# A four-stage attention kernel: work of one stage placed inside the end of the stage before

## The chip, the cores and the metric

The kernel runs on one core of one Trainium2 chip, as one program. The metric is the device time of one execution in microseconds; of the kernel before, three executions took 1231.0 to 1233.37 us, with a median of 1232.23.

## What is computed

Four layers follow each other on `x` (8 sequences of 128 tokens, 256 features); `ctx` has the same shape.

```python
# L0: 16 heads of width 8 over the channels; mean and deviation of the attended values
mean, ex2 = attn @ v, attn @ (v * v)
x = instance_norm(x) * sqrt(relu(ex2 - mean * mean)) + mean
# L1: queries from x, keys and values from [ctx, x], 16 heads of width 16, masked
out = rmsnorm(attention @ out_w + out_b + x) * postnorm_w
x = gelu_tanh(out @ w1 + b1) @ w2 + b2 + x                 # width 1024
# L2: two cross attentions on ctx, 16 heads of width 128, one extra learned key and value, then an MLP
for l in (1, 2):
    x = x + attention(layernorm(x), ctx) @ wo[l] + bo[l]
x = x + gelu(layernorm(x) @ fc1 + b) @ fc2 + b
# L3: cross attention on ctx, 16 heads of width 16, masked, then an MLP with gelu_tanh
x = x + attention(layernorm(x), ctx) @ wo + bo
x = x + gelu_tanh(layernorm(x) @ fc + b) @ proj + b
```

## The kernel before, in words

Each engine's program is written from the same lists of events, so that all five agree on the order. `att_order` (line 147) makes the list of an attention with narrow heads (L1 has 64 units, L3 has 32), `wide_order` (252) that of L2's two layers (16 head pairs of 8 units each), `mlp_order` (319) that of an MLP; `late` (229) moves some of VectorE's events behind the next score. The events are:

- `S` scores of a unit in PSUM, VectorE's maximum, ScalarE's Exp; `R` or the reciprocal on VectorE, the product with it on GpSimd (line 1629); `T` transposes of the probabilities (PE line 737 or 815); `PV` values; `OUT` and `WO` the output projection, added on VectorE.
- `dq`, `dk`, `dv`, `pq`, `pk` (L1, L3) and `q`, `k`, `v` (L2): projections.
- `nS`, `nX`, `nT`: the norm. `nS` gathers the statistics and takes the Sqrt on ScalarE (1013), `nX` writes the normalised rows to `XH` (1300, 1302), `nT` transposes two sequences (PE 641), scales them on ScalarE (1027, 1029) and splits them into a rounded part and a remainder in `ht` on VectorE (1316, 1317). `k` counts pairs of sequences, 0 to 3.
- `up` and `down`: the two MLP products of a pair of sequences. `up` is followed by the gelu (1165) and its split on VectorE (1501, 1502), four `up` to one `down`.
- `w`: a weight pack of 1024 columns is taken from the loading buffer `wraw` (two slots) by a cast on ScalarE (1004) and a remainder on VectorE (1266).

TensorE rounds its operands, so `three` (616) makes each dense product of three matmuls, of high and low parts. General products go through two PSUM banks in strict turn (`j_bank`, 603): the third one waits until the first has been read. Weights and operands live in one array `rs`, whose three regions A0, A1 and A2 change hands between the stages.

Between stages the order was this. At the end of an attention the units run out first; then come `nS` and `nX` for the first three pairs of sequences, the first MLP pack, the last `WO`, and `norm_end` (201), that is the last pair's norm and all four `nT`. Only then starts `up` of the first pair. In the MLP the last `down` comes before the next stage's norm is finished in the same way. A `down` waits until all four gelu splits of its pair are there:

```python
pe.wait_ge(m["lo"], (FT // 2) * (c + 1))
```

The last event of SP is one store of the whole output after the last `down`.

## Time and profile before

| | |
|---|---|
| median of three executions | 1232.23 us (1231.0 to 1233.37) |
| the profiled execution's own time | 1233.65 us |
| its span, first to last instruction | 1231.9 us |
| TensorE busy (matmuls) | 1081.0 us, 88% |
| VectorE, ScalarE, GpSimd busy | 747.5, 722.5, 321.1 us |
| mean granted clock of TensorE | 0.952 of full |
| HBM | 36.87 MB read, 1.05 MB written |

Times of rows are counted from the span's start. Busy time of TensorE counts overlapping matmuls once; a bracket behind a row gives the idle time just before it on that engine and what ended it. L0 lasts to some 213 us, the first attention to 372, its MLP to 434, the second stage to 975, its MLP to 1041, the third attention to 1162 and the last MLP to 1226.

### The profile page before, as it was taken

The numbers are of one execution on the slowest core, as the hardware profiler recorded it, in microseconds if no ns is written. First come the engines' busy times: TensorE is split into PE (matmuls) and PEld (weight loads), VectorE is DVE, ScalarE is ACT, GpSimd is POOL, SyncE is SP. The second block draws the span as 40 slices with busy tenths as digits, with TensorE's granted clock in tenths as the row PEclk, the third lists the DMA queues.
The fourth block names the chain that finished last, engine by engine and source line by source line (L and its number), as shares of the span: only waits on it lengthen the run. The fifth ranks groups of instructions, "written<-read, shape, count | busy, mean of one in ns | idle before, by whom it ended". The sixth has DMA issues, their size and how long they took to land. (4 is left out here: it accounts for less than half of the span.)

```text
span 1231.9 us, 23777 instructions
## 1 busy us (share of the span) xinstructions
PE 1081.0 (88%) x8224; PEld 952.6 (77%) x8224; DVE 747.5 (61%) x1763; ACT 722.5 (59%) x2096; POOL 321.1 (26%) x433
## 2 busy tenths in 40 slices
PE   3799995899968899999999989999999687789687
PEld 2577773777748878999999869999998587667487
DVE  4777674687876545555555745555555756666753
ACT  1577774778774346566656556656665433688631
POOL 5234335455440003111111112111111111343210
PEclk9799997999998999999999989999999899899799
DMA  6111110000002111010111111111100111000101
GB/s 198 24 29 44 44 28 34 2 2 1 1 19 75 44 45 40 30 35 34 40 44 65 44 43 44 44 44 44 44 35 19 35 35 35 1 2 2 35 1 35
DMA packets 20364, 43.65 MB, mean 35 GB/s; under 512 B 3347, under 2 KB 10773, under 8 KB 20246
## 3 DMA queue, kind: packets, MB, share of 16 engines
q1 hardware_dynamic: 20246, 42.12, 10.4%
q8 instruction: 68, 1.11, 0.4%
q14 instruction: 50, 0.41, 0.1%
HBM read 36.87 MB, written 1.05 MB: 31 GB/s over the span
## 5 line engine op out<-in xcount | busy, mean ns | idle before, releaser
L1629 POOL TENSOR_TENSOR pt<-pt,prec 128x256 f32<-128x256 f32 (+1 forms) x224 | 180.3, 805 | 647.2 <-DVE prec L1467 513.7
L618 PE MATMUL ps<-rs 128*128 128x256 f32 x480 | 147.0, 306 | 29.5 <-DVE rs L1502 19.4
L1127 ACT ACTIVATE pt<-ps,nmax 128x129 f32<-128x129 f32 x256 | 92.4, 367 | 96.1 <-DVE nmax L1459 95.4
L1266 DVE TENSOR_TENSOR rs<-wraw,rs 128x256 fp32r<-128x256 f32 (+2 forms) x108 | 69.3, 644 | 121.9 <-ACT rs L1004 121.2
L620 PE MATMUL ps<-rs 128*128 128x256 f32 x480 | 139.0, 290 | 0.0
L619 PE MATMUL ps<-rs 128*128 128x256 f32 x480 | 139.0, 290 | 0.0
L618 PE MATMUL ps<-ht,rs 128*128 128x256 f32 (+1 forms) x368 | 128.1, 348 | 2.1 <-ACT rs L1055 1.1
L1078 ACT ACTIVATE pt<-ps,nmax 128x256 f32<-128x256 f32 (+1 forms) x256 | 105.2, 423 | 33.8 <-DVE nmax L1405 25.4
L618 PEld LDWEIGHTS ps<-rs 128*128 128x128 f32 x480 | 95.2, 198 | 35.8 <-DVE rs L1502 12.7
L619 PE MATMUL ps<-ht,rs 128*128 128x256 f32 (+1 forms) x368 | 122.0, 331 | 0.0
L620 PE MATMUL ps<-ht,rs 128*128 128x256 f32 (+1 forms) x368 | 121.5, 330 | 0.0
L619 PEld LDWEIGHTS ps<-rs 128*128 128x128 f32 x480 | 95.5, 199 | 0.0
L1165 ACT ACTIVATE fs<-ps,col 128x256 f32<-128x256 f32 x96 | 40.4, 472 | 93.7 <-PE ps L620 88.1
L620 PEld LDWEIGHTS ps<-rs 128*128 128x128 f32 x480 | 95.2, 198 | 0.0
L1481 DVE SCALAR_TENSOR_TENSOR rs<-ps,col,rs 128x256 fp32r<-128x256 f32 x128 | 61.9, 483 | 46.7 <-ACT rs L1144 46.7
L618 PE MATMUL ps<-rs,ct 128*128 128x256 f32 x288 | 87.9, 305 | 1.3 <-DVE rs L1368 0.9
L1405 DVE TENSOR_REDUCE nmax<-ps 128x2 f32<-128x512 f32 (+1 forms) x96 | 66.2, 690 | 34.7 <-PE ps L729 29.2
L1576 DVE TENSOR_REDUCE nm<-ps 128x2 f32<-128x512 f32 x128 | 81.9, 680 | 8.1 <-PE ps L927 8.1
L806 PEld LDWEIGHTS ps<-fs 128*128 128x128 f32 x512 | 76.2, 191 | 10.2
L619 PE MATMUL ps<-rs,ct 128*128 128x256 f32 x288 | 81.6, 283 | 0.0
L620 PE MATMUL ps<-rs,ct 128*128 128x256 f32 x288 | 81.6, 283 | 0.0
L1206 ACT ACTIVATE pt<-ps 128x512 f32<-128x512 f32 x128 | 73.4, 598 | 12.8 <-PE ps L936 10.8
(198 smaller groups left out, 2989.9 us busy)
## 6 DMA issues: line engine op xcount, KB each, us to landing
wraw<-in_packs SPq DMA_DIRECT2D x55, 512.0 KB, 3.5
bvr<-in_l2rows SPq DMA_DIRECT2D x16, 256.0 KB, 4.6
rs<-rs SPq DMA_DIRECT2D x80, 32.0 KB, 1.9
ht<-rs SPq DMA_DIRECT2D x48, 32.0 KB, 1.9
row<-in_rows SPq DMA_DIRECT2D x2, 640.0 KB, 5.1
out<-X SPq DMA_DIRECT2D x1, 1024.0 KB, 4.5
X<-in_x SPq DMA_DIRECT2D x1, 768.0 KB, 7.5
XH<-in_ctx SPq DMA_DIRECT2D x1, 768.0 KB, 9.3
```

The source lines that it names most:

```text
L618: nc.tensor.matmul(dst, w[0], m[1], start=start, stop=False)
L619: nc.tensor.matmul(dst, w[1], m[0], start=False, stop=False)
L620: return nc.tensor.matmul(dst, w[0], m[0], start=False, stop=stop)
L806: last = nc.tensor.matmul(ps[:, S_BANK + g % 2, b * D:b * D + P + 1], qT[:, hh % 3, 2 * b2 + b, :], kT[:, hh % 3, 2 * b2 + b, :], start=Tr ...
L1078: last = nc.scalar.activation(prob[:, i % 3, h * keys:(h + 1) * keys], ps[:, SCORE_BANKS[ph][i % len(SCORE_BANKS[ph])], h * keys:(h + 1) * ...
L1127: last = nc.scalar.activation(prob[:, g % 3, k * D:k * D + P + 1], ps[:, S_BANK + g % 2, k * D:k * D + P + 1], ACT.Exp, bias=nmax[:, g % 4 ...
L1206: nc.scalar.activation(pt[:, i % L0_PTS, :], ps[:, L0_X[i % len(L0_X)], :], ACT.Exp, scale=Q0_SCALE).then_inc(Z["ex"], 1)
L1266: last = nc.vector.tensor_tensor(dst[1], src, f32(dst[0]), ALU.subtract)
L1405: nc.vector.tensor_reduce(nmax[:, i % 4, 0:nh], ps[:, SCORE_BANKS[ph][i % len(SCORE_BANKS[ph])], :].rearrange("p (h n) -> p h n", h=nh), A ...
L1481: nc.vector.scalar_tensor_tensor(cc[1][:, hd, two, :], ps[:, O_BANK + g % 2, 0:D].rearrange("p (b n) -> p b n", b=2), C(f"L2bv{p // PAIRS ...
L1576: nc.vector.tensor_reduce(nm[:, s % 3, im, 2 * p:2 * p + 2], ps[:, L0_S[i % len(L0_S)], :].rearrange("p (h n) -> p h n", h=2), AX.X, ALU.m ...
L1629: nc.gpsimd.tensor_tensor(pr, pr, prec[:, u % 4, 0:nh].unsqueeze(2).broadcast_to([P, nh, keys]), ALU.mult)\
```

## The change

`att_order`, `wide_order` and `mlp_order` yield the same products in another order. The norm is done in two groups of sequence pairs that depend on the norm (`GROUPS`), the first of them inside the attention that precedes; `norm_end` is gone. The MLP's packs are taken during the attention, three `up` stand in its tail, and `down` waits for each gelu split by itself. In the last head pair of each layer of the second stage the two heads take turns (`unit`), so that the output product of a pair of sequences can be made after every second unit. Keys, values and queries of the next stage stand between the steps of its norm. `rs` grows by a region A3; L3's selection matrices are loaded into `XH` and copied over the first MLP's weights during the second head pair. The scaled rows of a norm go to `XH`, not to a buffer of three slots. GpSimd waits for its rows pair by pair and clears the third stage's keys in two parts. The output is stored in four parts.

```diff
+STORED_AT = {n: i for i, n in enumerate(PACKS)}
+PACKS = [n for n in PACKS if not n.startswith("L3sel")]
...
-CHUNKS = (range(0, B // 2 - 1), range(B // 2 - 1, B // 2))
+GROUPS = {"L1r": ((0, 1, 2), (3,)), "L2n1": ((0, 1, 2), (3,)), "L2n2": ((0, 1), (2, 3)), "L2nm": ((0, 1), (2, 3)),
+          "L3n1": ((0, 1, 2), (3,)), "L3nm": ((0, 1), (2, 3))}
...
+    first, rest, sqrt = {"L1": (total - 24, total - 5, 6), "L3": (10, total - 3, 4)}[ph]
+    for k in range(PARTS):
+        put(first + 2 * k, "w", f"{ph}w1_0", k, 1)
+    put(rest, "w", f"{ph}w1_1", 0, 2)
+    put(rest + 1, "w", f"{ph}w1_1", 2, 2)
+    put(total - sqrt, "nS", after, 0)
+    put(total - sqrt + 1, "nX", after, 0)
+    for n, k in enumerate(GROUPS[after][0]):
+        put(total - sqrt + 2 + n, "nT", after, k)
+    for k in range(2):
+        put(total + k, "up", 0, k)
+        put(total + k, "w", f"{ph}w2_0", 2 * k, 2)
+        put(total + 5 + k, "w", f"{ph}w2_1", 2 * k, 2)
+    put(total + 4, "up", 0, 2)
+    if ph == "L3":
+        put(6, "nT", "L3n1", 2)
+        put(10, "nT", "L3n1", 3)
+        yield ("nT", "L3n1", 0)
+        yield ("dk", 0, 0)
+        yield ("nS", "L3n1", 1)
+        yield ("dv", 0, 0)
+        yield ("nX", "L3n1", 1)
+        yield ("dq", 0, 0)
+    else:
+        for _, e, k in dense:
+            yield (e, 0, k)
     for _, e, k in prep:
         yield (e, 0, k)
+    if ph == "L3":
+        yield ("nT", "L3n1", 1)
...
-                if it + 1 == c["iters"]:
-                    yield ("w", ph + "w1_1")
                 yield ("WO", it)
...
-        if u == total:
-            yield ("nS", after, 0)
-            yield ("nX", after, 0)
-            yield ("w", ph + "w1_0")
...
+        yield from more.get(u, [])
...
+def unit(g):
+    p, r = divmod(g, 8)
+    return (r % 2, r // 2) if p % PAIRS == PAIRS - 1 else divmod(r, 4)
...
+def gathered(p, b2):
+    return 8 * p + (2 * b2 + 2 if p % PAIRS == PAIRS - 1 else 4 + b2 + 1)
...
-            if 4 <= u < 8 and p + 1 < pairs:
+            if not last and 4 <= u < 8:
                 yield ("v", p + 1, u - 4)
+            if last and u in (4, 6) and p + 1 < pairs:
+                yield ("v", p + 1, u // 2 - 2)
...
-            if u >= 8:
-                yield ("WO", p, u - 8)
-            if u == 10:
+            if last and u >= 5 and u % 2:
+                yield ("WO", p, (u - 5) // 2)
+            if last and u == 8:
                 yield ("nS", norm, 0)
-            if u == 11:
+            if last and u == 9:
                 yield ("nX", norm, 0)
+            if last and u >= 10:
+                yield ("nT", norm, u - 10)
...
-            if 4 <= u < 8 and p == pairs - 1:
+            if p == 1 and u < 4:
+                yield ("sel", u)
+            if p == pairs - 1 and 4 <= u < 8:
                 yield ("w", f"L2w1_{u // 6}", 2 * (u % 2), 2)
...
+        if last:
+            yield ("nS", norm, 1)
+            if p + 1 < pairs:
+                yield ("q", p + 1, 0, 0)
+                yield ("nX", norm, 1)
+                yield ("q", p + 1, 1, 0)
+                yield ("v", p + 1, 2)
+                yield ("nT", norm, 2)
+                yield ("v", p + 1, 3)
+                yield ("nT", norm, 3)
+                yield ("q", p + 1, 0, 1)
+                yield ("q", p + 1, 1, 1)
+            else:
+                yield ("w", "L2w2_0", 0, PARTS)
+                yield ("w", "L2w2_1", 0, PARTS)
...
+    norms = {"L1": {(0, 3): [("nS", "L1r", 1)], (1, 0): [("nX", "L1r", 1), ("down", 0), ("nT", "L1r", 3)]},
+             "L2": {(0, 0): [("nX", "L2nm", 1)], (0, 1): [("nT", "L2nm", 2)], (0, 2): [("nT", "L2nm", 3)]},
+             "L3": {(0, 3): [("nS", "L3nm", 1)], (1, 0): [("nX", "L3nm", 1), ("down", 0), ("nT", "L3nm", 2)],
+                    (1, 1): [("nT", "L3nm", 3)]}}[name]
     for c in range(B // 2):
         for f2 in range(FT // 2):
-            yield ("up", c, f2)
-            if f2 == 0 and c > 0:
+            if name == "L2" or c > 0 or f2 == 3:
+                yield ("up", c, f2)
+            yield from norms.get((c, f2), [])
+            if f2 == 0 and (c > 1 or c == 1 and name == "L2"):
                 yield ("down", c - 1)
...
+            if (c, f2) in takes:
+                yield ("w", *takes[c, f2])
+    if name != "L3":
+        after = {"L1": "L2n1", "L2": "L3n1"}[name]
+        yield ("nS", after, 0)
+        yield ("nX", after, 0)
...
+        yield keys[0]
+        yield keys[1]
+        yield ("nT", "L2n1", 0)
+        yield keys[2]
+        yield ("nT", "L2n1", 1)
+    yield ("down", B // 2 - 1)
     if name == "L2":
         yield ("w", "L3att0", 0, PARTS)
         yield ("w", "L3att1", 0, PARTS)
...
     if name == "L1":
...
+        yield ("nS", "L2n1", 1)
+        yield keys[3]
+        yield ("nX", "L2n1", 1)
+        yield ("nT", "L2n1", 2)
+        yield ("v", 0, 0)
+        yield ("w", "L2p1_0", 0, PARTS)
+        yield ("v", 0, 1)
+        yield ("q", 0, 0, 0)
+        yield ("nT", "L2n1", 3)
+        yield ("q", 0, 1, 0)
+        yield ("v", 0, 2)
+        yield ("v", 0, 3)
+        yield ("q", 0, 0, 1)
+        yield ("q", 0, 1, 1)
...
+        A0, A1, A2, A3 = 0, 4096, 8192, 13312
+        ks = {"L1": [carve(rs, A0, [2048])[0], carve(rs, A0 + 2048, [2048])[0]], "L3": [carve(rs, A3, [2048])[0], carve(rs, A0, [2048])[0]]}
+        selw = sel[:, :, :].rearrange("p a b -> p (a b)")
...
-        aw = {"L1": awA, "L3": awB}
+        aw = {"L1": awA, "L3": awA}
...
-        pw = [carve2(rs, A0, [4, 512])[0], carve2(rs, A1, [4, 512])[0]]
+        pw = [carve2(rs, A1, [4, 512])[0], carve2(rs, A0, [4, 512])[0]]
...
+        mw1 = {"L1": first_layer(span(A3), selw), "L2": first_layer(span(A1), span(A1 + 2048)), "L3": first_layer(span(A0 + 2048), selw)}
+        mw2 = {"L1": carve2(rs, A0, [FT, D])[0], "L2": carve2(rs, A0, [FT, D])[0],
+               "L3": [carve(rs, A3, [FT, D])[0], carve(rs, A0, [FT, D])[0]]}
...
+                if name == "L2p1_0":
+                    sp.wait_ge(N["L2n1"]["lo"], B // 2)
+                    for k in range(2):
+                        sp.dma_start(XH[:, 4 * k:4 * k + 4, :].rearrange("p b d -> p (b d)"), packs[STORED_AT[f"L3sel{k}"]]).then_inc(s3_in, 16)
...
-            sp.wait_ge(M["L3m"]["out"], B // 2)
-            sp.dma_start(out.rearrange("b p d -> p b d"), X[:, :, :]).then_inc(out_done, 16)
-            sp.wait_ge(out_done, 16)
+            for c in range(B // 2):
+                sp.wait_ge(M["L3m"]["out"], c + 1)
+                sp.dma_start(out[2 * c:2 * c + 2].rearrange("b p d -> p b d"), X[:, 2 * c:2 * c + 2, :]).then_inc(out_done, 16)
+            sp.wait_ge(out_done, 16 * (B // 2))
...
-                    pe.wait_ge(m["lo"], (FT // 2) * (c + 1))
                     bank = j_bank()
                     for b in range(2):
                         for f in range(FT):
+                            if b == 0 and f % 2 == 0:
+                                pe.wait_ge(m["lo"], (FT // 2) * c + f // 2 + 1)
...
+                        if e[1].startswith("L2w1"):
+                            act.wait_ge(L["acc"], 4 * (2 * PAIRS - 1))
+                        if e[1].startswith("L2w2"):
+                            act.wait_ge(L["acc"], 4 * 2 * PAIRS)
...
+                    if e[1] == "L2p1_0":
+                        act.wait_ge(m["out"], B // 2)
+                    if e[1].startswith("L3att"):
+                        act.wait_ge(m["out"], B // 2)
...
+                    elif e[0] == "sel":
+                        dve.wait_ge(s3_in, 32)
+                        ins = nc.vector.tensor_copy(selw[:, 512 * e[1]:512 * (e[1] + 1)], XH[:, 2 * e[1]:2 * e[1] + 2, :].rearrange("p b d -> p (b d)"))
+                        if e[1] == 3:
+                            ins.then_inc(s3_ok, 1)
...
+                    dve.wait_ge(ybias, 4 * y + c + 1)
...
+                    if layer == 0 and u == 2 * B:
+                        nc.gpsimd.memset(ks["L3"][0].bitcast(F32), 0.0).then_inc(g_setup, 1)
...
-            pool.wait_ge(N["L2nm"]["xh"], B)
             for b in range(B):
+                if b % 2 == 0:
+                    pool.wait_ge(N["L2nm"]["xh"], b + 2)
                 add_row(X, "L2b2", b)
+            pool.wait_ge(M["L2m"]["lo"], 2 * FT)
+            zero_values()
             pool.wait_ge(M["L2m"]["out"], B // 2)
-            zero_keys("L3")
-            zero_values()
+            nc.gpsimd.memset(ks["L3"][1].bitcast(F32), 0.0).then_inc(g_setup, 1)
...
-            pool.wait_ge(N["L3nm"]["xh"], B)
             for b in range(B):
+                if b % 2 == 0:
+                    pool.wait_ge(N["L3nm"]["xh"], b + 2)
```

Line numbers of the changed kernel differ: `three` stands in 688 to 690, `nT` of TensorE in 711, transposes of probabilities in 812, values in 833 and 903, scores in 800, gelu in 1251, weight casts in 1081, Sqrt in 1090, Exp of a narrow attention in 1155, copies of transposed probabilities in 1164, the scaling of `nT` in 1102 and 1104.

TensorE at the end of the first attention, before: scores (725), transposes (737) and values (758) run out, then the output product (12 matmuls, the first three shown), then all four norm transposes, then `up` (operands `ht,rs`).

```order
L725 MATMUL ps<-rs 128x512
L737 MATMUL ps<-ident,pt 128x128 x4
L737 MATMUL ps<-ident,pt 128x128 x8
L758 MATMUL ps<-pt,fs 32x128 x8
L737 MATMUL ps<-ident,pt 128x128 x4
L758 MATMUL ps<-pt,fs 32x128 x8
L618 MATMUL ps<-rs 128x256
L619 MATMUL ps<-rs 128x256
L620 MATMUL ps<-rs 128x256
...
L641 MATMUL ps<-ident,XH 128x128 x16
L618 MATMUL ps<-ht,rs 128x256
```

The same place now:

```order
L812 MATMUL ps<-ident,pt 128x128 x4
L711 MATMUL ps<-ident,XH 128x128 x4
L800 MATMUL ps<-rs 128x512
L812 MATMUL ps<-ident,pt 128x128 x4
L711 MATMUL ps<-ident,XH 128x128 x4
L800 MATMUL ps<-rs 128x512
...
L711 MATMUL ps<-ident,XH 128x128 x4
L800 MATMUL ps<-rs 128x512
L812 MATMUL ps<-ident,pt 128x128 x4
L812 MATMUL ps<-ident,pt 128x128 x4
L688 MATMUL ps<-ht,rs 128x256
L688 MATMUL ps<-ht,sel 128x256
```

The norm transposes (711) of three pairs of sequences now stand between the last scores, and the first `up` stands ahead of the last values and of the output product.

ScalarE at the same place, before: the last Exp (1078) and copies (1087), then Sqrt with its table, the casts of both packs around the output's rounding (1093), the scaling (1029), and the gelu (1165) with its table.

```order
L1078 ACTIVATE pt,psums<-ps,nmax 128x256 x4
L1087 COPY pt<-ps 128x512
L1013 ACT_TABLE_LOAD
L1013 ACTIVATE sd<-sd,eps 128x6
L1004 CAST rs<-wraw 128x1024
L1087 COPY pt<-ps 128x512
L1093 CAST rs<-ps 128x512
L1004 CAST rs<-wraw 128x1024
L1013 ACTIVATE sd<-sd,eps 128x2
L1029 ACTIVATE fs<-ps,col 128x256 x8
L1165 ACT_TABLE_LOAD
```

And now:

```order
L1090 ACT_TABLE_LOAD
L1090 ACTIVATE sd<-sd,eps 128x6
L1155 ACT_TABLE_LOAD
L1155 ACTIVATE pt,psums<-ps,nmax 128x256 x2
L1081 CAST sel<-wraw 128x512
L1081 CAST sel<-wraw 128x512
L1104 ACTIVATE XH<-ps,col 128x256 x2
L1155 ACTIVATE pt,psums<-ps,nmax 128x256 x2
...
L1155 ACTIVATE pt,psums<-ps,nmax 128x256 x2
L1251 ACT_TABLE_LOAD
L1251 ACTIVATE fs<-ps,col 128x256 x2
L1081 CAST rs<-wraw 128x512
```

Sqrt, with a load of its table and one back to Exp, the two halves of a pack (`sel<-wraw`) and the scaling (1104) moved between the last Exp activations, and the gelu follows straight on the last of them. Over the whole program ScalarE has 17 table loads before and 23 now.

ScalarE from the second MLP into the third attention, before: the last gelus (1165), two packs, Sqrt for three pairs and for the last, all scaling (1027), then the projections (1049, 1055, 1071) and the first Exp.

```order
L1165 ACTIVATE fs<-ps,col 128x256 x28
L1004 CAST rs<-wraw 128x1024 x2
L1013 ACT_TABLE_LOAD
L1013 ACTIVATE sd<-sd,eps 128x6
L1013 ACTIVATE sd<-sd,eps 128x2
L1027 ACTIVATE pt<-ps,col 128x256 x8
L1049 ACTIVATE rs<-ps,col 128x256 x4
L1071 CAST rs<-ps 64x2x128 x2
L1078 ACT_TABLE_LOAD
L1078 ACTIVATE pt,psums<-ps,nmax 128x128 x4
```

And now:

```order
L1251 ACTIVATE fs<-ps,col 128x256 x26
L1090 ACT_TABLE_LOAD
L1090 ACTIVATE sd<-sd,eps 128x6
L1081 CAST rs<-wraw 128x1024 x2
L1102 ACTIVATE XH<-ps,col 128x256 x2
L1126 ACTIVATE rs<-ps,col 128x256 x2
L1090 ACTIVATE sd<-sd,eps 128x2
L1126 ACTIVATE rs<-ps,col 128x256 x2
L1148 CAST rs<-ps 64x2x128 x2
L1102 ACTIVATE XH<-ps,col 128x256 x2
L1155 ACT_TABLE_LOAD
L1155 ACTIVATE pt,psums<-ps,nmax 128x128 x4
```

The two packs come behind the Sqrt of the first group, which places them behind the last `down`; the scaling of one pair stands ahead of the projections instead of four.

## Rows read from the trace of the kernel before

**Rows 1.** Windows: length; busy PE, PEld, DVE, ACT, POOL (counts); PEclk; DMA share, GB/s

```profile
346.00:389.00 43.00, 30.34 (x263) 24.55 (x263) 33.16 (x77) 29.07 (x77) 11.18 (x11) 0.84 0.15 48
389.00:433.70 44.70, 40.90 (x325) 40.29 (x326) 23.68 (x52) 12.80 (x27) 0.00 (x0) 0.96 0.19 62
433.70:457.70 24.00, 21.10 (x115) 18.03 (x114) 11.02 (x23) 10.44 (x21) 0.00 (x0) 0.93 0.10 33
692.40:723.80 31.40, 27.13 (x151) 22.47 (x150) 19.36 (x54) 14.87 (x35) 1.23 (x2) 0.89 0.01 2
951.20:996.80 45.60, 30.03 (x197) 27.45 (x197) 34.99 (x79) 23.26 (x59) 11.73 (x14) 0.85 0.14 44
996.80:1041.40 44.60, 41.05 (x326) 40.45 (x327) 22.49 (x50) 12.72 (x26) 0.00 (x0) 0.96 0.08 27
1041.40:1061.60 20.20, 10.80 (x63) 9.28 (x61) 14.64 (x27) 7.47 (x17) 6.98 (x2) 0.75 0.00 0
1061.60:1147.00 85.40, 73.04 (x665) 60.18 (x666) 55.05 (x137) 75.16 (x315) 35.73 (x37) 0.98 0.01 2
1147.00:1181.80 34.80, 22.07 (x168) 18.04 (x167) 27.64 (x55) 19.22 (x45) 11.17 (x11) 0.80 0.09 31
1181.80:1226.30 44.50, 40.90 (x324) 40.09 (x324) 15.03 (x27) 9.24 (x22) 0.00 (x0) 0.96 0.01 1
```

**Rows 2.** Timeline of PE: start us, us, what, at half and full clock

```profile
428.40 0.41 PE L618 MATMUL ps<-rs 128*128 128x256 f32 x1
428.62 0.41 PE L619 MATMUL ps<-rs 128*128 128x256 f32 x1
...
432.11 0.28 PE L620 MATMUL ps<-rs 128*128 128x256 f32 x1
432.23 0.28 PE L618 MATMUL ps<-rs 128*128 128x256 f32 x1
```

**Rows 3.** Timeline of PE: waits ahead of down products

```profile
401.59 0.39 PE L618 MATMUL ps<-rs 128*128 128x256 f32 x1 [0.97 <-DVE rs L1502]
...
413.96 0.39 PE L618 MATMUL ps<-rs 128*128 128x256 f32 x1 [0.71 <-DVE rs L1502]
...
1035.33 0.39 PE L618 MATMUL ps<-rs 128*128 128x256 f32 x1 [2.12 <-DVE rs L1502]
```

**Rows 4.** Timeline of PE: last head pair of the second stage

```profile
958.70 0.44 PE L815 MATMUL ps<-ident,pt 128*128 128x128 f32 x2 [1.62 <-POOL pt L1629]
```

**Rows 5.** Timeline of ACT: end of the first attention

```profile
361.36 1.28 ACT L1013 ACT_TABLE_LOAD   x1
362.65 0.30 ACT L1013 ACTIVATE sd<-sd,eps 128x6 f32<-128x6 f32 x1
...
374.62 2.46 ACT L1029 ACTIVATE fs<-ps,col 128x256 f32<-128x256 f32 x6
```

**Rows 6.** Timelines of ACT and DVE: one weight pack cast and rounded

```profile
368.38 1.05 ACT L1004 CAST rs<-wraw 128x1024 fp32r<-128x1024 f32 x1
...
369.53 1.23 DVE L1266 TENSOR_TENSOR rs<-wraw,rs 128x1024 fp32r<-128x1024 f32 x1 [0.32 <-ACT rs L1004]
```

**Rows 7.** Timelines of DVE and POOL: splits alone and beside bias adds

```profile
378.39 0.42 DVE L1316 CAST ht<-fs 128x512 fp32r<-128x512 f32 x1
378.85 0.69 DVE L1317 TENSOR_TENSOR ht<-fs,ht 128x512 fp32r<-128x512 f32 x1
...
1171.21 0.96 DVE L1316 CAST ht<-fs 128x512 fp32r<-128x512 f32 x1
...
1167.89 8.05 POOL L1653 TENSOR_TENSOR X<-X,row 128x256 f32<-128x256 f32 x8 [16.46 <-DVE XH L1302]
```

**Rows 8.** Timeline of POOL: a memset of 4096 columns

```profile
1042.14 3.51 POOL L1633 MEMSET rs<- 128x4096 f32 x1 [51.02 <-DVE X L1509]
```

**Rows 9.** Page, DMA issues: KB each, us from issue to landing

```profile
wraw<-in_packs SPq DMA_DIRECT2D x55, 512.0 KB, 3.5
out<-X SPq DMA_DIRECT2D x1, 1024.0 KB, 4.5
```

225 lines of the change are left out of this document (102 added, 123 removed).

## The prediction

> **What bounds the kernel now.** I read the page's slices first, then one table of windows laid over the joins between the stages, then the timelines of single engines inside those joins. Inside the stages TensorE is the bound; the time is lost where one stage hands over to the next. The table [rows 1] has a row for each join and each MLP block. A join's loss is its length less TensorE's busy time, plus what the half clock costs. Idle: 43.00 - 30.34 = 12.7 us in the join from the first attention into its MLP; 3.8 in the first MLP; 2.9 from there to the second stage; 4.3 between its two layers; 15.6 at its end; 3.6 in the second MLP; 9.4 on the way into the third attention; 12.7 at its end; 3.6 in the last MLP; and 5.6 from its end at 1226.3 to the span's 1231.9, for the output. That is 74 us.
>
> The clock column tells the rest. The matmul of 256 columns starts every 0.21 us where the granted clock is 0.50 (1.2 GHz) and every 0.12 us where it is 1.00 (2.4 GHz) [rows 2], so a busy microsecond at the half clock loses 45%. A mean clock of 0.84 over 43 us is 13.8 us at half. The stretches at half follow those in which TensorE waited.
>
> In the MLP blocks each "down" product starts with a wait for the last rounding of the gelu output: 0.97 us, 0.71 us, and 2.12 us ahead of the last of each block [rows 3].
>
> **The change, part by part.** The order rows show what moves: norms, roundings and first MLP products of finished sequences go between units of attention that are still running, and the second stage's keys, values and queries stand around the last norms. The sum of TensorE's work stays. So each join is costed as a pool (idle plus clock loss), less what the move puts back.
>
> 1. *End of the first attention.* Pool: 12.7 + 13.8 x 0.45 x 0.70 (its busy share) = 17.1 us. Put back: the six last units now also carry, on ScalarE, a load for Sqrt and one back to Exp (2 x 1.28 us [rows 5]), the cast of the second weight pack (1.05 [rows 6]) and three norm groups (2.46 [rows 5]), 6.1 us; on VectorE the pack's low part (1.23 [rows 6]), 1.7 us of normalising and three splits of 0.42 + 0.69 [rows 7], 6.2 us. VectorE was 77% and ScalarE 68% busy over the whole join [rows 1], more in its first third, so I charge the whole 6 us to the scores. Of the chain after the last output product (add, statistics, Sqrt, normalise, transpose, scale, split) some 3.5 us stay uncovered, since only two up products stand ahead of the first down. Gain 17.1 - 6 - 3.5 = 7.6, taken as **7.5 us**.
>
> 2. *End of the third attention.* Pool: 12.7 + 13.9 x 0.45 x 0.63 = 16.6 us. Put back 2 x 1.28 + 1.05 + two norm groups at 0.82 = 5.2 us on ScalarE, which is the fuller engine there, and 3.5 again: **8 us**.
>
> 3. *End of the second stage.* Pool: 15.6 + 13.7 x 0.45 x 0.66 = 19.7 us. Two output products move up into the stalls of the last units (TensorE waits 1.62 us for GpSimd there [rows 4], in about four units), and half the sequences are normalised before the last two. What stays: some 3 us of those stalls; about 5 us because the second layer's weights can be cast only when the last output product is added up, so two casts, the load for Gelu and the first gelu (1.05 x 2 + 1.28 + 0.82, a gelu pair being as wide as a norm pair) stand ahead of the third up product; 2 us since GpSimd's eight bias adds, 8.05 us, stretch VectorE's casts from 0.42 to 0.96 us [rows 7], and now start earlier in the join; and 1.7 of the last chain. Gain **8 us**.
>
> 4. *Between the layers.* Pool: 4.3 + 6.9 x 0.45 x 0.86 = 7.0. The cover (two value, two key, two query products) is longer than the chain; **5 us**. *First MLP into second stage*: 2.9 + 3.4 x 0.45 x 0.88 = 4.2; **3.5 us**.
>
> 5. *Into the third attention.* Pool: 9.4 + 10.1 x 0.45 x 0.53 = 11.8 us. Before, the weights were cast under the last down; now both packs are cast after it (2 x 1.05 on ScalarE, then 2 x 1.23 less overlap on VectorE, some 4 us in which TensorE has one transpose group). Against that only one norm group stands ahead of the first scores, not four. Gain **7 us**.
>
> 6. *Waits ahead of down.* Each becomes four waits, pair by pair, and 18 matmuls of 0.12 us (2.1 us) stand ahead of the last pair. The first down of each block lies in a join above; nine remain: 0.97 + 0.71 + 2.12 in the first block and twice 0.71 + 0.71 + 2.12 in the others [rows 3], **10.9 us**. Each block also has some 3.5 us at half clock (0.96 in [rows 1]), 4.8 us of loss in all, of which I take **3**.
>
> 7. *Output.* 1 MB landed 4.5 us after its issue, 512 KB in 3.5 [rows 9]. By that slope the last quarter needs 3.0: **1.5 us**.
>
> Costs elsewhere. The third attention had ScalarE at 75.2 of 85.4 us [rows 1]; it gets three norm groups (2.5) and four quarter casts (1.4): I charge **3.5** of the 3.9 us. The first attention gets the same quarter casts, **1 us**. One GpSimd memset of half the old 3.51 us [rows 8] now stands between two probability products of the second stage, on which TensorE waits: **1 us** of 1.75. GpSimd's bias adds stand in the join after the third attention as well [rows 7]: **2 us**. The copies of the last selection onto VectorE (four, at most 0.7 us each by the split's width) cost nothing: VectorE is about half busy there and TensorE the bound. That selection's two loads wait on SP for the last norm of the second stage, with the pack of the second head pair queued behind them. Three transfers of 512 KB at 3.5 us, overlapping, are in well before the third unit, which lies some 12 us behind that norm; were they not, 3 us once.
>
> The trace of before never shows two products in a row that straddle a running attention, so the put-back of parts 1 and 2 is bounded: between 0 (all of it in idle slots) and 11 us each (each engine's added work in series, 6.1 + 6.2, less a little). I take values near the middle, since ScalarE and VectorE were two thirds to nine tenths busy.
>
> Sum: 7.5 + 8 + 8 + 5 + 3.5 + 7 + 10.9 + 3 + 1.5 = 54.4; less 3.5 + 1 + 1 + 2 = 7.5; 46.9 us. The profiled execution took 1233.65 us, 1.4 above the median of 1232.23. 1233.65 - 46.9 = 1186.8; I say **1186**.
>
> One rule speaks against the change. The added loads count six (17 before, 23 now), and in the trace a load takes 1.28 us and the Sqrt starts 1.29 us after the load did [rows 5], so nothing else is paid. The Trainium skill ("ScalarE: Activation LUTs", section on what ACT_TABLE_LOAD costs) adds a drain of 1.38 us to each switch. By that, the four loads among attention units would cost 5.5 us more and the time would be about 1192; by this rule, the trace does not agree.
>
> **Rivals.**
> *The tails pay for what they save* (20%). If the added ScalarE and VectorE work in the last units delays the scores by the upper bound, parts 1 and 2 bring nothing: 1186 + 15.5 = about 1202. For it: the two engines' busy shares and the in-order queues. Against: part of that work only moves from the same tail.
> *The clock stays up* (14%). The pools hold 76 us at the half clock; at a busy share of 0.7 they lose 24 us, of which the sum takes about 12. If the covers keep it at full everywhere, 12 us more: 1174. For it: it fell only behind waits. Against: tails stay half idle.
> *The order moves, the waits do not* (10%). If a weight cast, a buffer or the j banks (two only, filled in strict order) hold the moved products, the joins keep seven tenths of their loss; only part 6, the output and some cover remain: 1186 + 0.7 x 39 = about 1213.
> *Slower* (5%). Place: the three MLP blocks. If breaking the long idle stretches into many short waits left the clock at half through the MLP blocks, each of their 384 matmuls would take 0.093 us more; from 504 matmuls at half the whole gain is gone. Two blocks cost 768 x 0.093 = 71 us: 1258. Against it: these blocks had waits of 0.7 to 2.1 us already [rows 3] and a mean clock of 0.96 [rows 1].
>
> **Numbers.** Forecast 51% (1179 to 1196), the others as above. The range goes from 1170 (most of the clock case) to 1212 (the first rival and half of the third); about 17% is left out. A measurement of this kernel tells about 0.2% from no change. Faster: 51 + 20 + 14 + 9; same 1; slower 5.
>
> **What would show it.** Right: the down rows without a wait; TensorE idle under 6 us in the joins of parts 1, 2 and 5; six more loads of 1.28 us, with scores before them later by 4 to 6 us; the third attention 3 to 4 us longer; mean clock of the joins above 0.9. Wrong: a join as long as before, with TensorE waiting for VectorE's casts or ScalarE's loads; the third attention longer by over 6 us; clock rows below 0.8 inside an MLP block; a wait for a pack near the second head pair.

## The result, and the profile after

The changed kernel took 1210.37 us, the median of four executions (1208.11 to 1210.8), against 1232.18 us for four of the kernel before in the same comparison: a ratio of 0.9819, interval 0.9802 to 0.9836. That is 21.8 us less. The forecast was 1186, so less than half of the gain came; 1210.4 lies inside the range, near its upper end. The profiled execution has a span of 1208.2 us against 1231.9 and a mean clock of 0.964 against 0.952. One execution in this study, of the kernel with two moves in the first attention's tail, took 2057.5 us and is left out of that kernel's median.

Windows of the changed kernel over the same joins and blocks, in the order of [rows 1], without the second and the third MLP block and the third attention (columns as there):

```profile
346.00:382.40 36.40, 26.93 (x241) 21.94 (x239) 28.43 (x62) 26.83 (x69) 10.35 (x10) 0.91 0.12 37
382.40:424.40 42.00, 39.43 (x307) 37.60 (x307) 27.36 (x64) 19.69 (x43) 0.00 (x0) 1.00 0.08 26
424.40:446.40 22.00, 20.25 (x134) 17.97 (x135) 10.26 (x21) 6.76 (x13) 0.00 (x0) 1.00 0.17 56
680.80:712.20 31.40, 25.18 (x153) 20.92 (x153) 19.28 (x55) 16.07 (x39) 1.84 (x3) 1.00 0.01 1
940.30:985.90 45.60, 31.05 (x190) 28.83 (x190) 32.12 (x74) 22.07 (x55) 9.92 (x14) 0.81 0.14 47
1022.60:1042.70 20.10, 11.64 (x74) 10.66 (x73) 13.51 (x31) 6.75 (x14) 3.80 (x2) 0.83 0.16 52
1128.10:1162.50 34.40, 25.94 (x214) 21.09 (x211) 24.58 (x54) 24.47 (x73) 9.99 (x10) 0.85 0.05 16
```

Each window ends at the same mark as its counterpart (first down, first scores), so idle time and clock compare, while where a join begins is a choice. At the end of the second stage 14.6 us are idle against 15.6, at a lower clock (0.81 against 0.85). Into the third attention it is 8.5 against 9.4, at the end of the third attention 8.5 against 12.7, at the end of the first 9.5 against 12.7. So 0.9 to 4.2 us of idle time went per join, of 9.4 to 15.6.

To compare kernels piece by piece I use rows of VectorE as marks: the sum of an output or down product, and the first maximum of a layer's scores. A "stretch" below is the time between two such marks in the profiled execution. In the changed kernel some of them are:

```profile
388.82 0.68 DVE L1600 TENSOR_TENSOR X<-ps,X 128x512 f32<-128x512 f32 x1
447.11 0.43 DVE L1550 TENSOR_REDUCE nmax<-ps 128x2 f32<-128x258 f32 x1 [2.54 <-PE ps L881]
712.91 0.43 DVE L1550 TENSOR_REDUCE nmax<-ps 128x2 f32<-128x258 f32 x1 [3.61 <-PE ps L881]
991.99 0.69 DVE L1600 TENSOR_TENSOR X<-ps,X 128x512 f32<-128x512 f32 x1 [3.73 <-PE ps L690]
1044.76 0.69 DVE L1491 TENSOR_REDUCE nmax<-ps 128x4 f32<-128x512 f32 x1
1169.44 0.68 DVE L1600 TENSOR_TENSOR X<-ps,X 128x512 f32<-128x512 f32 x1
1204.91 0.69 DVE L1600 TENSOR_TENSOR X<-ps,X 128x512 f32<-128x512 f32 x1 [3.95 <-PE ps L690]
```

They are the first down sum of the first MLP, the first maxima of the second stage's two layers, the first down sum of the second MLP, the first maximum of the third attention, and the first and last down sums of the last MLP. Between such marks most stretches repeat to 0.1 us from one execution to the next where the program is the same. Those across a join in which the granted clock changes differ by 1 to 2 us now and then. Starting from the sum of the first attention's third output product (342.6 us in the kernel before, 339.3 to 343.4 in all the others, whatever they change), the stretches take, in us:

| up to | before | down waits alone | down waits and output | changed | best version |
|---|---|---|---|---|---|
| first down, first MLP | 52.4 | 50.9 | 50.0 | 48.6 | 47.4 |
| first maximum, second stage | 63.3 | 59.0 | 59.0 | 58.3 | 58.3 |
| first maximum, second layer | 266.2 | 265.7 | 265.4 | 265.8 | 264.6 |
| first down, second MLP | 279.9 | 276.0 | 276.0 | 279.1 | 272.4 |
| first maximum, third attention | 57.8 | 56.7 | 54.9 | 52.8 | 48.4 |
| first down, last MLP | 127.1 | 123.8 | 122.7 | 124.7 | 122.9 |
| last down | 37.1 | 33.0 | 33.0 | 35.5 | 35.5 |
| sum | 883.7 | 865.0 | 860.9 | 864.7 | 849.5 |

All but the first and the changed kernel are experiments below. The two columns with the down waits hold the same program but for where the output is stored, and still differ by 4.1 us in sum, most of it into the third attention and behind it (over the latter the granted clock was 0.90 in one and 0.96 in the other). So much can two profiled executions differ, and what the moved work is worth in a join is known no better than these two columns agree. The table already says what the study found: the changed kernel gains 18.9 us between these marks, one small part of the change gains 18.6 or 22.7 by itself, and the moved work gains in some joins what it loses in others.

### The profile page after: what moved, and what is told of

Read it like the earlier page. It is cut to its first block, busy times and chain, and to the rows that moved or that the text cites. A ratio compares the mean times of both kernels' runs of the same rounds, so it can differ in the third digit from the quotient of the medians.

```text
span 1208.2 us, 23834 instructions
## 1 busy us (share of the span) xinstructions
PE 1073.6 (89%) x8224; PEld 947.2 (78%) x8224; DVE 747.4 (62%) x1777; ACT 731.9 (61%) x2114; POOL 319.4 (26%) x435
## 4 chain that ended last, share of the span: by engine, by line
PE 69%; DVE 13%; ACT 9%; issue 6%; POOL 3%; DMA 0%; SPq 0%; DVEq 0%; ACTq 0%; POOLq 0%
PE ps L688 15%; PE ps L689 14%; PE ps L690 14%; PE ps L903 4%; PE ps L881 4%; PE ps L1026 2%; ACT pt L1155 2%; PE ps L890 2%; PE ps L812 2%; DVE nm L1667 2%; PE ps L1013 2%; PE ps L1004 1%; PE ps L833 1%; PE ps L769 1%; DVE nmax L1491 1%
## 5 line engine op out<-in xcount | busy, mean ns | idle before, releaser
L688 PE MATMUL ps<-rs 128*128 128x256 f32 x480 | 144.7, 301 | 8.7 <-DVE rs L1572 3.9
L689 PE MATMUL ps<-rs 128*128 128x256 f32 x480 | 137.4, 286 | 0.0
L690 PE MATMUL ps<-rs 128*128 128x256 f32 x480 | 137.4, 286 | 0.0
L688 PE MATMUL ps<-ht,rs 128*128 128x256 f32 (+1 forms) x304 | 108.6, 357 | 8.5 <-DVE X L1511 3.1
L688 PEld LDWEIGHTS ps<-rs 128*128 128x128 f32 x480 | 93.8, 195 | 13.0 <-DVE rs L1572 6.2
L689 PE MATMUL ps<-ht,rs 128*128 128x256 f32 (+1 forms) x304 | 102.1, 336 | 0.0
L690 PE MATMUL ps<-ht,rs 128*128 128x256 f32 (+1 forms) x304 | 101.9, 335 | 0.0
L689 PEld LDWEIGHTS ps<-rs 128*128 128x128 f32 x480 | 93.9, 196 | 0.0
L690 PEld LDWEIGHTS ps<-rs 128*128 128x128 f32 x480 | 93.6, 195 | 0.0
```

Source lines behind the costliest of these rows:

```text
L688: nc.tensor.matmul(dst, w[0], m[1], start=start, stop=False)
L689: nc.tensor.matmul(dst, w[1], m[0], start=False, stop=False)
L690: return nc.tensor.matmul(dst, w[0], m[0], start=False, stop=stop)
```

## The experiments

### The waits ahead of down, alone

The kernel before, with

```diff
-                    pe.wait_ge(m["lo"], (FT // 2) * (c + 1))
                     bank = j_bank()
                     for b in range(2):
                         for f in range(FT):
+                            if b == 0 and f % 2 == 0:
+                                pe.wait_ge(m["lo"], (FT // 2) * c + f // 2 + 1)
```

> The kernel before with one edit: a down product waits for each gelu split by itself (part 6 of the change alone). My sum had 10.9 us for nine waits, 3 us of clock, and some 3.5 us more for the first down of each block, which it counted in the joins: by the prediction's terms 1232 - 11 to 17, so 1215 to 1221. Theory A (what was off in the forecast lies at the joins, part 6 was sized right): 1216 to 1221, every wait at L1502 ahead of a down gone and the MLP blocks at full clock. Rival B (part 6 was sized too large too: the wait only moves to the last pair of splits, or to the next up): 1224 to 1229, with waits of 0.3 us or more left inside the down products.

Measured: 1212.2 us (ratio 0.9836, interval 0.9809 to 0.9863). Far more than either theory had. One line of the waits by releaser in the kernel before holds most of the reason (waited for: us in total, times, longest). Three of its twelve waits stand ahead of the first down of an MLP, and the two largest of all are among them:

```profile
PE ps L618 <- DVE rs L1502: 19.4, 12, 3.7
```

```profile
996.77 0.36 PE L618 MATMUL ps<-rs 128*128 128x256 f32 x1 [3.51 <-DVE rs L1502]
1181.78 0.55 PE L618 MATMUL ps<-rs 128*128 128x256 f32 x1 [3.70 <-DVE rs L1502]
```

I had counted nine waits of 10.9 us and left the three first ones (1.25, 3.51 and 3.70, together 8.5) in the pools of the joins. With the edit no wait for a gelu split is left; the first downs of the second and third MLP wait 1.38 and 1.35 us for a weight remainder instead:

```profile
984.84 0.35 PE L618 MATMUL ps<-rs 128*128 128x256 f32 x1 [1.38 <-DVE rs L1267]
1165.36 0.36 PE L618 MATMUL ps<-rs 128*128 128x256 f32 x1 [1.35 <-DVE rs L1267]
```

The other reason is the clock. In the kernel before, each MLP block has a piece at half the clock behind one of these waits: matmuls 0.21 us apart in [rows 2], and 16 of them from 997.21 to 1000.41 behind the wait of 3.51 us. The window of that piece, kernel before:

```profile
996.80:1004.00 7.20, 7.20 (x48) 7.20 (x49) 0.75 (x2) 0.00 (x0) 0.00 (x0) 0.76 0.05 18
```

and the three MLP blocks of this kernel:

```profile
384.50:425.00 40.50, 40.05 (x330) 39.27 (x328) 24.99 (x55) 14.03 (x31) 0.00 (x0) 1.00 0.21 65
984.80:1026.00 41.20, 39.59 (x328) 39.04 (x328) 25.23 (x54) 13.56 (x28) 0.00 (x0) 1.00 0.13 43
1165.00:1205.00 40.00, 38.95 (x324) 38.60 (x324) 18.26 (x33) 10.09 (x24) 0.00 (x0) 1.00 0.01 2
```

With the waits the half clock is gone from the blocks. Three blocks of 16 matmuls at 0.093 us each make some 4.5 us (an estimate), where the forecast took 3. Over the whole profiled execution the mean clock is 0.952 in both kernels, since other stretches had more of the half clock in this one.

A restart costs something at full clock too. Windows from the first to the third down sum of the first MLP, kernel before and this one:

```profile
395.00:420.00 25.00, 23.31 (x194) 22.91 (x194) 12.95 (x24) 6.72 (x16) 0.00 (x0) 1.00 0.16 54
```

```profile
390.20:413.00 22.80, 22.80 (x194) 22.80 (x194) 12.95 (x25) 6.73 (x16) 0.00 (x0) 1.00 0.18 59
```

The clock is 1.00 in both, and TensorE is busy throughout now. The gain is 2.2 us where the two waits were 1.7: each restart had cost another 0.25 us, with 194 matmuls busy for 23.31 us and not 22.80.

### The output in four parts, alone

The kernel before with the four stores of the change and nothing else.

> The kernel before with one edit: the output is stored in four parts, each as soon as its pair of sequences is added (part 7 alone). Forecast term 1.5 us: 1230.7. In the changed kernel the way from the last matmul to the span's end is 3.3 us against 5.6, so theory A says 2.3 us: 1229.9. Rival B (the shorter end there came from something else): under 0.5 us, 1232.

Measured: 1229.4 us against 1231.3 (0.9982, interval 0.9966 to 0.9997): 1.9 us. Theory A. The page gives the landing of each quarter as 2.1 us, where I had extended a slope to 3.0 (the row is the same in this kernel and the changed one; 4.5 for the whole in [rows 9]):

```profile
out<-X SPq DMA_DIRECT2D x4, 256.0 KB, 2.1
```

### Both small parts together

> The kernel before with the down waits (part 6) and the output in four parts (part 7) together, nothing else of the change. Alone they took 1212.2 and 1229.4 us. Theory A (these two small parts are the measured gain of the whole change; all its moved work adds nothing to them): 1209 to 1212, no different from the changed kernel's 1210.4. Rival B (the moved work earns something that the two do not): 1213 or more.

Measured: 1207.7 us, a ratio of 0.9798 (0.9773 to 0.9823), against the changed kernel's 0.9819 (0.9802 to 0.9836). The intervals overlap, and the small version is ahead if anything. It gains 24.4 us where the two parts alone gained 19.1 and 1.9, so such sums are good to some 3 us. By this kernel the moved work as a whole loses 2.6 us, by the sum of the parts alone it gains 0.8: nothing that can be told from zero. Its column is in the table above.

### The waits taken back in the changed kernel

> The changed kernel with one edit undone: a down product again waits for all four gelu splits of its pair (part 6 taken out). The kernel before with part 6 alone took 1212.2 us, nearly what the whole change took (1210.4). Theory A (the waits ahead of down are the change, and the rest of it is worth some 2 us, the output's): this kernel comes out at 1226 to 1231. Rival B (the two overlap: the moved work fills the same waits, so either alone would do): 1212 to 1220.

Measured: 1225.7 us (0.9949, interval 0.9931 to 0.9967), 15 us slower than the changed kernel, just under the edge of theory A. So the moved work with the output is worth 6 us as long as the old waits stand: 6.2 and 19.1 for the down waits alone are 25.3, the whole change has 21.8, and the two share 3.5 us. The place where they meet is the first down: with three up products in the tail its old wait is 1.32 us in the last MLP, where it was 3.70, and in the second TensorE waits 0.92 us there, not 3.51 (in the first it is 1.89, where it was 1.25). The half clock comes back with the old waits too: it is 0.88 ahead of the last down of the second and third MLP, 1.00 there in the changed kernel.

### One wait at a time

In the changed kernel the joins have new waits, each behind work that the change put ahead in an in-order queue. The experiments on them differ from the changed kernel by less than their executions can show: but for the output products one step later, each ratio's interval overlaps the changed kernel's 0.9802 to 0.9836. They are read by their stretches, and a stretch counts only beside those of the kernels with nothing edited there. TensorE:

```profile
950.92 0.47 PE L890 MATMUL ps<-ident,pt 128*128 128x128 f32 x1 [2.68 <-POOL pt L1718]
957.88 0.48 PE L890 MATMUL ps<-ident,pt 128*128 128x128 f32 x1 [2.40 <-POOL pt L1718]
...
1026.10 0.63 PE L711 MATMUL ps<-ident,XH 128*128 128x128 f32 x4 [1.17 <-DVE XH L1386]
1031.56 0.55 PE L688 MATMUL ps<-ct,rs 128*128 128x256 f32 x1 [4.83 <-DVE rs L1350]
```

The largest is at 978.72: the transposes of the third pair wait 5.36 us for VectorE's normalising. VectorE there:

```profile
971.99 0.17 DVE L1377 COPY sd<-mv 128x4 f32<-128x4 f32 x1
973.53 2.36 DVE L1350 TENSOR_TENSOR rs<-wraw,rs 128x1024 fp32r<-128x1024 f32 x2 [1.37 <-ACT rs L1081]
976.56 0.43 DVE L1593 CAST rs<-fs 128x512 fp32r<-128x512 f32 x1 [0.67 <-ACT fs L1251]
977.02 0.69 DVE L1594 TENSOR_TENSOR rs<-fs,rs 128x512 fp32r<-128x512 f32 x1
977.63 0.17 DVE L1380 RECIPROCAL sd<-sd 128x4 f32<-128x4 f32 x1
977.83 1.79 DVE L1386 TENSOR_SCALAR XH<-X,mv,sd 128x256 f32<-128x256 f32 x4
```

The statistics were ready at 972.2 and Sqrt ended at 972.5, but two weight remainders, a table load for Gelu, the first gelu and its split stand ahead of the normalising at 977.83.

**Weight casts behind the second and third up product.**

```diff
-                yield ("w", "L2w2_0", 0, PARTS)
-                yield ("w", "L2w2_1", 0, PARTS)
...
-             "L2": {(0, 0): [("nX", "L2nm", 1)], (0, 1): [("nT", "L2nm", 2)], (0, 2): [("nT", "L2nm", 3)]},
+             "L2": {(0, 0): [("nX", "L2nm", 1)], (0, 1): [("nT", "L2nm", 2), ("w", "L2w2_0", 0, PARTS)], (0, 2): [("nT", "L2nm", 3), ("w", "L2w2_1", 0, PARTS)]},
```

> The changed kernel with the casts of the second MLP's down weights (two of 1024 columns) moved from ahead of its first gelu to behind the second and third up product. In the changed kernel TensorE waits 5.36 us ahead of the transposes of the third pair, for VectorE, which does the two remainders (2.36 us) and a gelu split first. Queue theory (what stands ahead in VectorE's and ScalarE's order is what the chain waits for): that wait falls to under 1.5 us and 2.5 to 4.5 us are gained from the last maximum of the second stage to the first down: 1206 to 1208. Rival (the loss only moves: the first down then waits for its weights): the wait goes, the first down waits 2 us or more instead, and the time stays within 1 us of 1210.4.

Measured: 1211.7 us (0.9830, interval 0.9805 to 0.9856). The wait fell only from 5.36 to 3.98 us. The stretch from the last maximum to the first down is 38.3, but 38.5 to 39.2 in kernels with nothing edited there, so at most some 0.9 us came of it. Neither theory: the first gelu and its split still stand ahead of the normalising, so a second thing was as late as the first.

**Normalising of the first group ahead of the third output product.**

> The changed kernel with the normalising of the first two pairs (nX, group 0) put ahead of the values and the third output product of the last head pair, in both layers of the second stage. In the changed kernel it starts 5 us after its Sqrt, and TensorE waits 2.06 us for it. Queue theory: the 2.06 us wait goes, 1 to 2 us gained at the end of the second stage and up to 1 us between its layers: 1207.5 to 1209.5. Rival (normalising of 1.79 us now stands ahead of the rounding of the values that the last output products wait for, so the loss moves to these): 1210 to 1212.

Measured: 1208.5 us (0.9807, interval 0.9784 to 0.9830). From the second layer's first maximum to the first down 275.2 us, against 279.1 in the changed kernel and 278.0 to 279.1 in all with nothing edited there, but 1.0 us more between the layers, where the same event stands ahead of other work. The rival holds at one place and the queue theory at the other.

**Third attention's casts ahead of the last down.**

> The changed kernel with the two weight casts of the third attention taken ahead of the last down product, not behind its sum. In the changed kernel TensorE waits 4.83 us for their remainder. Queue theory: the wait falls under 1.5 us, and 2.5 to 4.5 us are gained between the last down but one and the first scores: 1206 to 1208. Rival (VectorE's remainders, 2.36 us, now stand ahead of the last down's sum and the statistics, so the last pair's norm is later by as much and the first scores wait for that): the wait goes but the time stays within 1 us of 1210.4.

Measured: 1209.4 us (0.9811, interval 0.9785 to 0.9837). The wait of 4.83 us became one of 3.54 us, now for the last down's sum, which reads one of the two PSUM banks that these products share.

```profile
1030.89 0.55 PE L688 MATMUL ps<-ct,rs 128*128 128x256 f32 x1 [3.54 <-DVE X L1598]
```

From the third down of the second MLP to the first down of the last, 153.2 us against 154.7 (154.3 to 155.6 with nothing edited there). Between the two theories, nearer the rival.

**The first attention's tail.** The norm group starts two units earlier, its transposes stand two units apart, and the down pack's casts come behind the output product.

```diff
-    first, rest, sqrt = {"L1": (total - 24, total - 5, 6), "L3": (10, total - 3, 4)}[ph]
+    first, rest, sqrt = {"L1": (total - 24, total - 5, 8), "L3": (10, total - 3, 4)}[ph]
+    apart = {"L1": 2, "L3": 1}[ph]
...
-        put(total - sqrt + 2 + n, "nT", after, k)
+        put(total - sqrt + 2 + apart * n, "nT", after, k)
...
-        put(total + k, "w", f"{ph}w2_0", 2 * k, 2)
+        put(total + (5 if ph == "L1" else 0) + k, "w", f"{ph}w2_0", 2 * k, 2)
```

> The changed kernel with two moves in the first attention's tail: the norm of the first three pairs starts two units earlier and its three transposes (each with a split of 1.1 to 1.9 us on VectorE) stand two units apart, not one; and the casts of the first down pack come behind the output product. In the changed kernel TensorE waits 3.45 us and 2.25 us for copies of transposed probabilities that stand behind such splits and a remainder on VectorE. Queue theory: those waits fall to 1 us or less and 2 to 4 us are gained ahead of the first down: 1206.5 to 1208.5. Rival (VectorE's total in the tail is the bound, so waits come elsewhere, or the first down waits for its pack): within 1 us of 1210.4.

Measured: 1208.5 us, the median of three executions (0.9793, interval 0.9761 to 0.9826). The stretch to the first down is 46.1 us, not 48.6, as the queue theory has it. Its mechanism held in part: the two waits fell to 1.56 and 1.81 us, but the first down waits 1.62 us for its pack, which the rival named, and idle time fell only from 11.2 to 10.4 us. TensorE's busy time fell from 37.42 to 35.74 us with the granted clock at 0.96 and not 0.93, and that is the larger part of the gain.

**Output products of the last head pairs one step later.**

```diff
+            if last and u in (6, 8, 9, 11):
+                yield ("WO", p, (6, 8, 9, 11).index(u))
...
-            if last and u >= 5 and u % 2:
-                yield ("WO", p, (u - 5) // 2)
```

> The changed kernel with the first two output products of the last head pair one step later: the first behind the next scores, the second ahead of the transposes on which TensorE waits 2.40 us, the third ahead of the next ones. VectorE then takes both last maxima ahead of these sums and statistics. Queue theory: the waits of 2.68 and 2.40 us shrink to about 1 us each, the stretches to the last maximum return to 235.5 and 239.0, and 2 to 4 us are gained over the two layers: 1206.5 to 1208.5. Rival (the chain from scores over Exp and GpSimd's product is what takes the time, and the order on VectorE does not matter): within 1 us of 1210.4.

Measured: 1206.7 us (0.9774, interval 0.9751 to 0.9797). The first layer's stretch to its last maximum is 235.5 us again, the second's 237.6, its end 37.2 against 39.2 (38.5 to 39.2 with nothing edited there). Of the edits in this section it is the only one whose time by itself is clear of the changed kernel's. As the queue theory has it, though the wait of 2.68 us is still 1.52, and that of 2.40 is replaced by 1.69 and 1.23.

**The last head pairs as before.** The two heads no longer take turns, the output products follow the scores, the first norm group stands behind the third of them.

> The changed kernel with one part undone: in the last head pair of each layer of the second stage the heads no longer take turns, the four output products stand behind the scores again, and the norm of the first two pairs behind the third of them, with its transposes. In the changed kernel the stretch from the first maximum of a layer to the last is 0.9 us longer than before (236.4 against 235.5, 239.9 against 239.0) and TensorE waits 2.68 and 2.40 us for probabilities. Queue theory (the output products' sums and statistics stand ahead of the maxima of the last scores, and cost what they save): the two layers return to 235.5 and 239.0, the joins get longer by about as much, and the time is within 1.5 us of 1210.4. Rival (taking turns is what still earns something there): 1213 to 1218.

Measured: 1213.8 us (0.9832, interval 0.9809 to 0.9855). From the last maximum of the first layer to the first of the second, 35.8 us against 29.4, and 1.3 less inside the first layer; from the second layer's first maximum to the first down 277.4 us against 279.1 (278.0 to 279.1 with nothing edited there). So taking turns earns 5 us between the layers and loses 0.6 to 1.7 at the end: mostly the rival.

### VectorE beside GpSimd's memsets

In the changed kernel GpSimd clears the third stage's values as soon as the last gelu split is done. POOL and DVE:

```profile
1021.08 3.52 POOL L1726 MEMSET fs<- 128x4096 f32 x1 [38.85 <-DVE rs L1594]
```

```profile
1021.47 3.15 DVE L1377 COPY sd<-mv 128x6 f32<-128x6 f32 x1
```

A copy of six columns, 0.17 us elsewhere, takes 3.15 us and ends with the memset. Sqrt, normalising and the transposes follow it.

```diff
+            pool.wait_ge(M["L2m"]["lo"], 4)
+            nc.gpsimd.memset(fs[:, 0:2048], 0.0)
+            nc.gpsimd.memset(fs[:, 3072:4096], 0.0)
             pool.wait_ge(M["L2m"]["lo"], 2 * FT)
-            zero_values()
+            nc.gpsimd.memset(fs[:, 2048:3072], 0.0).then_inc(vzero, 1)
```

> The changed kernel with one edit: GpSimd clears the third stage's values in three pieces, two of them (2048 and 1024 columns) early in the second MLP and the last 1024 columns where all 4096 were cleared at once. In the changed kernel the copy of 6 statistics columns on VectorE, 0.17 us elsewhere, takes 3.15 us beside that memset (3.52 us), and Sqrt, the normalising and the transposes into the third attention follow it. Theory A (VectorE's copy stands still until GpSimd's memset is over): the copy takes at most 1 us, the first transpose of the third stage's norm comes without its 1.17 us wait, and since the weights' casts come behind the last down anyway, 1 to 2 us are gained: 1208.5 to 1209.5. Rival B (the copy's length is a record's artefact, or the wait for the weights swallows all): the copy stays long, or it is short and the time stays within 0.5 us of 1210.4.

Measured: 1209.3 us (0.9811, interval 0.9783 to 0.9838). The copy takes 0.58 us, and the stretch from the third down of the second MLP to the first down of the last takes 151.5 us; in the six kernels of this study that have the change's memset and nothing edited there it lay between 154.3 and 155.6. The wait of 1.17 us is gone and that of 4.83 us for the casts is 4.01. Theory A's mechanism, at twice its price by the stretch. The copy:

```profile
1021.03 0.58 DVE L1377 COPY sd<-mv 128x6 f32<-128x6 f32 x1
```

The kernel before has the same loss, twice, which I had read past:

```profile
1043.18 2.49 DVE L1293 COPY sd<-mv 128x2 f32<-128x2 f32 x1
...
1047.02 2.39 DVE L1316 CAST ht<-pt 128x512 fp32r<-128x512 f32 x1 [1.34 <-ACT pt L1027]
```

There I cut each memset into four:

> The kernel before with each memset of 4096 columns on GpSimd (third stage's keys and values, and the same helpers in the first stage) cut into four of 1024 columns, at the same place, so GpSimd's work is the same. In the kernel before, a copy of 2 statistics columns took 2.49 us and a rounding of 512 columns 2.39 us on VectorE beside the two memsets on the way into the third attention, against 0.17 and 0.42 elsewhere. Lock theory (such a VectorE instruction stands still until the GpSimd instruction that holds the shared port is over): both take at most 0.9 + 0.4 us, and 2 to 4 us go from the stretch between the third down of the second MLP and the first maximum of the third attention, 33.1 us before. Rival (the two engines share bandwidth over the whole of GpSimd's work): the durations fall little, and the stretch stays at 33.1.

Measured: 1228.7 us against 1232.1 (0.9971, interval 0.9954 to 0.9988); the stretch named is 31.4 us. VectorE in this kernel, beside 7.8 us of memsets in pieces:

```profile
1041.26 0.82 DVE L1293 COPY sd<-mv 128x2 f32<-128x2 f32 x1
...
1043.41 0.72 DVE L1316 CAST ht<-pt 128x512 fp32r<-128x512 f32 x1 [1.34 <-ACT pt L1027]
1044.17 0.69 DVE L1317 TENSOR_TENSOR ht<-pt,ht 128x512 fp32r<-128x512 f32 x1
...
1044.97 2.12 DVE L1302 TENSOR_SCALAR XH<-X,mv,sd 128x256 f32<-128x256 f32 x2
```

The copy stands for one piece (0.82 us) where it stood for 2.49, the rounding 0.72 where it took 2.39. But the normalising that had come behind the memsets (0.74 us for two) now runs beside them and takes 2.12, and the rounding behind it 1.25 and not 0.42. A remainder with two inputs and the plain 0.69 us is not touched. So the lock theory holds, and cutting the memset gave 1.7 of some 4.3 us back; moving most of it away, in the changed kernel, gave 3.2.

The Trainium skill ("SBUF — State Buffer", section "Who interferes with whom") says that VectorE in its two-port mode and GpSimd share a port pair that is locked for a whole instruction, and that the later one fully blocks. By that rule, the trace agrees: 3.15 us for a copy that began 0.39 us after a memset of 3.52.

### GpSimd's bias adds later

```diff
-                    pool.wait_ge(N["L2nm"]["xh"], b + 2)
+                    pool.wait_ge(N["L2nm"]["lo"], 2 + b // 4 * 2)
```

(and the same for the last MLP)

> The changed kernel with GpSimd's bias adds ahead of the second and third MLP later: four after the split of the second pair, four after that of the fourth, so they no longer stand beside the normalising and splits of the last norm. In the changed kernel roundings beside them take 0.95 us, not 0.43, and remainders 1.10, not 0.69. My forecast charged 2 us for them at each of two joins. Lock theory: 0.5 to 2 us gained at the end of the second stage and as much after the third attention: 1207 to 1209.5. Rival (VectorE has slack at these moments, or the gelu splits now meet the adds instead): within 1 us of 1210.4.

Measured: 1209.3 us (0.9807, interval 0.9773 to 0.9841); the two stretches (last maximum of the second stage and of the third attention, each to the first down behind it) 39.0 and 28.8 us, against 39.2 and 28.9. The rival. Roundings of 0.95 us beside the adds are real, and cost nothing there.

### Table loads

> The kernel before with six Sqrt activations of one column added on ScalarE between Exp groups of the third attention (after units 6, 10, 14, 18, 22, 26), each with a table load for itself and one back: 12 loads more, whose result nobody uses. Theory A (a load costs its 1.28 us and nothing else): 12 x 1.28 + 6 x 0.22 = 16.7 us of ScalarE, of which up to 10 us fit into its idle time in that attention, so the time rises by 7 to 17 us, to 1239 to 1249, and the activation behind each load starts 1.3 us after it. Rival B (a further drain of 1.38 us for each load, as the Trainium skill, ScalarE: Activation LUTs, states): 33 us of ScalarE, a rise of 23 to 33 us, 1255 to 1265, with gaps of over 1 us ahead of each load or behind it. Rival C (the third attention absorbs it, as my forecast of 3.5 us for 3.9 us of added work would not allow): a rise under 4 us.

Measured: 1244.0 us (1.0099, interval 1.0067 to 1.0132), 12.7 us more. ScalarE around one of the added pairs:

```profile
1089.62 1.28 ACT L1084 ACT_TABLE_LOAD   x1
1090.92 0.20 ACT L1084 ACTIVATE extra<-eps 128x1 f32<-128x1 f32 x1
...
1092.23 1.28 ACT L1079 ACT_TABLE_LOAD   x1
1093.53 0.37 ACT L1079 ACTIVATE pt<-ps,nmax 128x128 f32<-128x128 f32 x1
```

Each activation starts 1.30 us after its load, and the cast before the second load ends where the load begins. The attention got 10.4 us longer (96.1 against 85.7) for 16.7 us of added ScalarE work, so two thirds of such work were paid there. Theory A. The drain of 1.38 us that the Trainium skill states ("ScalarE: Activation LUTs", section on what ACT_TABLE_LOAD costs) is not in this trace, and the time would have been 1255 or more with it by the estimate of rival B.

### A version that keeps the change and beats both

Four edits together, three of them those above and the last one new: values cleared in pieces, third attention's casts ahead of the last down, normalising of the first group earlier (in the last layer alone), and that of the second group ahead of the first up product, with the down casts behind the second and third.

> The changed kernel with four edits together: the memset of the values in pieces (alone 3.2 us less from the second MLP's third down to the last), the casts of the third attention ahead of the last down, the normalising of the first group earlier in the last layer alone (the second stage's end was 3.4 us shorter with it, the join between its layers 1.0 longer), and the normalising of the second group ahead of the first up product, with the down weights' casts behind the second and third. Queue theory (each removes work from ahead of the chain, at different places, so the gains add): 3.2 + 3.4 + 1 to 3 for the others, so 1201 to 1204. Rival (one join's gain is another's wait): 1206 to 1210.

Measured: 1198.2 us, ratio 0.9703 (0.9681 to 0.9725), better than the queue theory's 1201 to 1204. From the last maximum of the second stage to the first down 33.3 us, not 39.2: with casts and gelu both behind it, the wait of 5.36 us is one of 1.81, where moving the casts alone had left 3.98. (The normalising of the first group alone had given 36.7.) So the wait was there because of what stood ahead of the normalising.

> All edits of the four-edit kernel (1198.2 us), with the first attention's tail as in the kernel with two moves there (2.5 us less ahead of the first down), and the output products of the last head pairs one step later (3.3 us less over the second stage and its end with it alone). Queue theory (gains at different places add; at the second stage's end the two edits meet and share): 2.5 + 0.9 + 0.9 + 0 to 2 more, so 1192 to 1195. Rival (the output product's step and the earlier normalising exclude each other there): 1195.5 to 1198.

Measured: 1197.9 us, 0.9719 (0.9692 to 0.9746): no different. In the profiled executions its stretches sum to 849.5 us against 852.8, but at the second stage's end the two edits share one gain (272.4 against 273.2 us), and the first join gained 1.2 us here, not 2.5. The first down waits for its pack, but it did so with the two moves alone as well; what differs is the granted clock over the join, 0.93 here and 0.96 there, with TensorE busy for 37.06 and 35.74 us. The wait here:

```profile
382.73 0.36 PE L690 MATMUL ps<-rs 128*128 128x256 f32 x1 [1.62 <-DVE rs L1350]
```

The rival, in the end. Its windows over the joins at the second stage's end and into the third attention:

```profile
949.70:984.50 34.80, 26.62 (x177) 24.93 (x177) 25.76 (x60) 16.55 (x34) 10.62 (x12) 0.86 0.15 46
1007.30:1032.90 25.60, 20.80 (x152) 19.55 (x150) 19.32 (x48) 12.55 (x23) 2.76 (x2) 0.93 0.12 42
```

against, in the changed kernel, between the same marks:

```profile
952.80:992.00 39.20, 28.14 (x177) 26.69 (x177) 26.75 (x61) 16.59 (x34) 7.92 (x10) 0.81 0.13 41
1014.80:1044.80 30.00, 21.52 (x152) 20.04 (x150) 20.98 (x49) 12.62 (x23) 5.32 (x2) 0.89 0.11 36
```

In the first, idle time fell from 11.1 to 8.2 us, in the second from 8.5 to 4.8; the clock rose with it in both.

## Why the prediction was wrong

The sum had 15.4 us for parts 6 and 7 and 31.5 us net for the moved work. Together parts 6 and 7 brought 24.4 us (21.0 by the sum of the two alone), and the moved work beside them nothing that can be told from zero. The direction and the wide range held; the gain was 21.8 us for 46, and its two shares were wrong in opposite ways.

**Parts 6 and 7** were too small. The output gave 1.9 us for 1.5. The one-line edit of the down waits gave 19.1 for 13.9. Between the first and the last down of the three MLPs the blocks got 4.3, 2.6 and 4.1 us shorter, 11.1 in all for nine waits costed at 10.9, and 1.5 of these are clock. The clock term, 3 us, was right in kind and if anything low: the half clock of all three blocks went, worth some 4.5. What was left out is the three waits ahead of the first downs, 8.5 us, which were put into the joins' pools as if the moved work would earn them. The one-line edit earned all but some 2.7 us of them.

**Parts 1 to 5 as pools.** This is the step that failed: "each join is costed as a pool (idle plus clock loss), less what the move puts back". The put-back was summed as busy time of an engine, but VectorE and ScalarE take their work in order (the Sqrt of the second group ended at 972.5 us and its normalising began at 977.83, behind two weight remainders and a gelu split), and what counts is which instruction stands ahead of the one that TensorE waits for. Where two figures are given for the small parts, they are those of the two columns above.

1. End of the first attention, forecast 7.5: the stretch fell by 3.8 us, 2.4 or 1.5 of it with the small parts alone. Two waits, of 3.45 and 2.25 us, are for copies of transposed probabilities behind splits and a remainder on VectorE.
2. End of the third attention with the attention itself, 8 less 3.5 and 2: 2.4 us, as forecast, but 4.4 or 3.3 with the small parts alone. So the figure was met by luck, through the first down's wait, and the move lost 1 to 2 us. The attention from its first to its last maximum takes 95.8 us, not 85.7, and what follows to the first down 28.9, not 41.4. Charging ScalarE's added work was right in kind (two thirds of it were paid in the experiment with loads).
3. End of the second stage, forecast 8: 0.8 us, against 3.9 without the move in both columns, so it lost 3. The forecast named the two casts and the gelu ahead of the third up product but priced them at 5 us of a pool of 19.7; it missed that they stand ahead of the second group's normalising, and that sums and statistics of early output products stand ahead of the last maxima.
4. Between the layers, forecast 5: 0.4 us over the layer and the join, no more than with the small parts alone. Taking turns earns 5 there, but only against a version with the rest of the change. First MLP into the second stage, 3.5: 0.7 us beyond the small parts.
5. Into the third attention, forecast 7: 5.0 us from the first down of the second MLP on, 2.9 or 1.1 of them with the small parts, so 2.1 to 3.9. "Some 4 us" for the casts was close to the wait (4.83), but the copy held by the memset, 3.2 us, was in no term, and the kernel before had such holds in its rows too.
6. The last MLP, in no term of the sum: from its first to its last down 33.0 us with the small parts, in both columns, and 35.5 with the moved work. That is 2.5 us lost.

**Costs elsewhere.** The bias adds (2 us after the third attention, 2 more inside part 3) cost nothing. The last selection's loads and copies and GpSimd's memset in the first layer (1 us) held nobody up: the layers differ from before only by the 0.9 us that went with the output products' place. Table loads cost their 1.28 us each, as said.

**The rivals.** "The tails pay for what they save" is what happened at the end of the second stage and of the third attention, and the first attention's tail kept 1.4 to 2.3 us of its 7.5. "The order moves, the waits do not" gave 1213, the nearest number, and was right in part. It named a weight cast: the wait of 4.83 us is for one, and that of 5.36 stands behind two, though not these alone. It named the banks: one wait of the changed kernel, 3.10 us ahead of an up product in the third attention's tail, ends with the sum of an output product, which reads a bank. The rest was the order of VectorE's own queue, which it did not name. But it kept part 6 at its size in the sum, and its number is near because that part was too small and the moved work earned nothing.

**The signs.** Of the signs of being right, the down rows are without a wait for a split, and there are six loads more. Idle time in the joins of parts 1, 2 and 5 is 9.5, 8.5 and 8.5 us, not under 6, and the clock was 0.81 to 0.85 in three joins, not above 0.9. Of the signs of being wrong, the third attention came out longer by over 6 us (10.1), though what stands behind it is shorter by 12.5. No MLP block fell to half the clock.

What stays open: why the best version still spends 8.2 us idle at the second stage's end; how much of the last MLP's 35.5 us against 33.0 is the two transpose groups that now stand in it and how much its waits (1.03 and 0.58 us); and how much of the 9.5 us between the kernel with both small parts (1207.7) and the four edits (1198.2) needs the moved work, since the memset could be moved in the kernel before as well. None of these was tried.

## What to carry to other kernels

Before costing an overlap, add up one releaser's waits over the whole program: a wait for "all four" that can be four waits may be worth as much as the restructuring around it (19.1 us of 21.8 here). When work moves into an in-order queue, ask for each moved instruction what stands behind it and who waits for that; a sum of busy time does not tell, and two late things in series hide each other until both are moved. Before reading an edit's gain from one profiled execution, see how far the same stretch moves in kernels that leave it alone. And look at a small VectorE instruction that takes as long as a GpSimd one beside it.

## What the runs showed of the hardware

A copy of two to six columns on VectorE took 2.49 and 3.15 us, not 0.17, beside a GpSimd memset that had begun first. With the memset cut into pieces of 1024 columns the copy took 0.82 us, but then other VectorE instructions met the next pieces (2.12 us for 0.74, 1.25 for 0.42). TensorE's restart after a wait of 0.71 or 0.97 us cost about 0.25 us beyond the wait, at full clock; behind a wait of 3.51 us 16 matmuls ran at half the clock, and with the waits gone the three MLP blocks were at 1.00. A store of 256 KB landed in 2.1 us where 1 MB takes 4.5.
